# Dealing of token rows by indirect transfers: pairs on two semaphores in place of runs of sixteen

## What is computed

```python
logits = flat @ Wr                                   # 4096 x 8
probs = softmax(logits); topk_p, topk_i = top_k(probs, 2)
topk_p = topk_p / topk_p.sum(-1)
capacity = ceil(n * 2 / 8 * 1.25)                    # 1280
order = argsort(-score, axis=1)[:, :capacity]        # each expert's tokens, heaviest first
dispatch = flat[order]
expert_out = (silu(dispatch @ w1) * (dispatch @ w3)) @ w2 * weight_sel
routed = zeros.at[order].add(expert_out)
out = routed + (silu(flat @ s1) * (flat @ s3)) @ s2  # h + this
```

## Time and profile before

| | us |
|---|---|
| median of 3 runs | 2147.89 (2139.88 to 2156.07) |
| profiled execution | 2143.08, its span 2141.3 |
| granted TensorE clock, mean | 0.939 of full speed |
| busy: TensorE | 1915.5 (89%) |
| busy: VectorE, ScalarE, GpSimd | 1141.0, 739.1, 426.9 |

### The profile page before, as it was taken

The page is one execution under the profiler, slowest core; times in us unless marked ns, Lnnn a source line. Parts: engine busy times, 40 slices in busy tenths (PEclk is TensorE's granted clock), DMA queues, the critical chain, the costliest instruction groups (busy, mean ns, idle before and its releaser), DMA issues. The chain is left out here.

```text
span 2141.3 us, 28066 instructions
## 1 busy us (share of the span) xinstructions
PE 1915.5 (89%) x10075; PEld 1209.1 (56%) x10075; DVE 1141.0 (53%) x2777; ACT 739.1 (35%) x1248; POOL 426.9 (20%) x567
## 2 busy tenths in 40 slices
PE   4985569999999999779999996898799999999997
PEld 2442432444444444446666663555358888888886
DVE  5898668666666765368778873474112222222221
ACT  1434014455545555445655551211011111111111
POOL 5200211022102210201111110103711222222222
PEclk9987568999999999889999997899899999999999
DMA  2610022112111210000000000101221222122321
GB/s 64 223 48 0 1 80 57 52 38 60 53 52 38 60 50 18 26 11 6 6 6 6 6 6 26 74 1 40 80 73 40 69 59 60 32 61 61 68 39 18
DMA packets 68748, 94.75 MB, mean 44 GB/s; under 512 B 15386, under 2 KB 57662, under 8 KB 66337
## 3 DMA queue, kind: packets, MB, share of 16 engines
q1 hardware_dynamic: 52482, 77.19, 11.3%
q0 software_dynamic: 16128, 15.76, 4.3%
HBM read 54.96 MB, written 39.47 MB: 44 GB/s over the span
## 5 line engine op out<-in xcount | busy, mean ns | idle before, releaser
L1028 DVE TENSOR_REDUCE row_max<-c_ps_m 128x1 f32<-128x512 f32 x384 | 253.0, 687 | 112.1 <-PE c_ps_m L1198 106.7
L1376 ACT ACTIVATE e<-c_ps_s 128x512 f32<-128x512 f32 x384 | 216.5, 596 | 220.8 <-PE c_ps_s L1214 220.1
L2675 DVE TENSOR_TENSOR e_f<-e_ps_u,e_gate 128x512 f32<-128x512 f32 x120 | 83.0, 692 | 271.5 <-ACT e_gate L2957 179.1
L2476 POOL DMA_INDIRECT out<-m_o,m_row_of x80 | 125.7, 1572 | 281.9 <-issue 252.7
L2892 PE MATMUL e_ps_o<-m_w,e_f 128*128 128x192 f32 x960 | 162.6, 326 | 0.9 <-DVE e_f L2675 0.9
L2892 PEld LDWEIGHTS e_ps_o<-m_w,e_f 128*128 128x128 f32 x960 | 158.1, 190 | 3.3 <-DVE e_f L2675 1.3
L1198 PE MATMUL c_ps_m<-c_kT,qT 96*128 96x512 bf16 x384 | 150.0, 397 | 10.4 <-DVE row_max L1028 10.2
L1214 PE MATMUL c_ps_s<-qT,c_kT 97*128 97x512 bf16 x384 | 144.6, 386 | 13.1 <-ACT e L1376 5.6
L2957 ACT ACTIVATE e_gate<-e_ps_g 128x512 f32<-128x512 f32 x120 | 71.7, 597 | 242.3 <-PE e_ps_g L2866 162.3
L2860 PE MATMUL e_ps_g<-m_xT,m_w 128*128 128x256 f32 x480 | 129.6, 392 | 1.0 <-DVE h L2507 1.0
L2860 PE MATMUL e_ps_u<-m_xT,m_w 128*128 128x256 f32 x480 | 123.2, 379 | 0.0
(11 more groups left out here) (459 smaller groups left out, 3748.4 us busy)
## 6 DMA issues: line engine op xcount, KB each, us to landing
dealt<-x SPq DMA_DIRECT2D x8, 1290.0 KB, 15.1
m_x<-dealt SPq DMA_DIRECT2D x40, 258.0 KB, 2.7
spread<-parts SPq DMA_DIRECT2D x24, 384.0 KB, 2.3
qT<-spread SPq DMA_DIRECT2D x144, 64.0 KB, 2.5
c_kT<-spread SPq DMA_DIRECT2D x144, 64.0 KB, 2.5
m_w<-in_w13e SPq DMA_DIRECT2D x8, 1152.0 KB, 5.1
m_w<-in_w2e SPq DMA_DIRECT2D x8, 576.0 KB, 6.1
out<-h SPq DMA_DIRECT2D x8, 384.0 KB, 3.9
```

The costliest lines, as they stand in the source:

```text
L1028: dve.tensor_reduce(row_max[:, n // J, n % J:n % J + 1], ps_m[:, n % 2, :], AX_X, ALU.max)\
L1376: act.activation(e[:, n % LIVE_E, :], ps_s[:, n % 2, :], ACT.Exp, scale=QSCALE).then_inc(e_ready, 1)
L2476: pool.indirect_dma_start(out=out_rows, out_offset=bass.IndirectOffsetOnAxis(ap=row_of[:, n % 2, r:r + 1], axis=0), in_=o[:, n % 2, r, :], ...
L2675: dve.tensor_tensor(fe[:, n % 2, 2 * i:2 * i + 2, :], ps_ue[:, q % 2], gate_e[:, q % 2], ALU.mult)\
```

## The change

In place of one semaphore there are two, and pairs of transfers use them in turn: transfers 0 and 1 the first, 2 and 3 the second, 4 and 5 the first again. Before each pair, GpSimd waits until the pair before the previous one has landed, so that at most four transfers are under way. The waits after 16 and after 48 transfers are gone; at the end of each half (k) GpSimd waits for both semaphores. SyncE waits for both too. The count, order and content of the transfers are the same.

```diff
-        scattered = kit.pool_dma_sem("s_scattered")
+        scattered = [kit.pool_dma_sem(f"s_scattered{w}") for w in range(2)]
...
-            sp.wait_ge(scattered, 2 * NB * 16)
+            for w in range(2):
+                sp.wait_ge(scattered[w], NB * 16)
...
                 for b in range(NB):
+                    pair = (k * NB + b) // 2
+                    if b % 2 == 0:
+                        past(pool, scattered[pair % 2], pair // 2 * 32)
                     pool.indirect_dma_start(
                         out=dealt, out_offset=bass.IndirectOffsetOnAxis(ap=slot[:, k, b:b + 1], axis=0),
                         in_=x1[:, b, :], in_offset=None, bounds_check=SLOTS - 1, oob_is_err=False
-                    ).then_inc(scattered, 16)
-                    if (b + 1) % (NB // 2) == 0:
-                        pool.wait_ge(scattered, (k * NB + b + 1) * 16)
-            pool.wait_ge(scattered, 2 * NB * 16)
+                    ).then_inc(scattered[pair % 2], 16)
+                for w in range(2):
+                    pool.wait_ge(scattered[w], (k + 1) * NB // 2 * 16)
```

## The result

| | kernel before | kernel after |
|---|---|---|
| median | 2151.35 us (4 runs, 2139.88 to 2156.07) | 2175.64 us (4 runs, 2172.65 to 2177.42) |
| ratio | | 1.0105, interval 1.0075 to 1.0134 |
| profiled execution, span | 2143.08, 2141.3 us | 2172.65, 2170.9 us |

The change costs 24.3 us between the medians and 29.6 us between the two spans. The profiled execution of the kernel before was one of its quicker ones (2143.08 against a median of 2151.35), which is the main reason why the two differ. The forecast was 2151 us with a range up to 2168; the time lies above it. Lines behind the edit stand 3 to 4 further down in the changed kernel: the transfer is L2454, the gate L2934, the residual L2510, the output matmuls L2753.

What follows compares the result with a forecast made beforehand. TensorE was taken to bound the kernel, with the shared expert 36.0 us late only during GpSimd's dealing. Dealing 0, waits 0, lateness +3 on the 2147.89 us median gave 2151 us, range 2106 to 2168.

Steps and rivals of the forecast that it cites:

- Slack and length of the dealing: GpSimd's 64 row transfers: 84.1 us instead of 88.1, ending near 1559; rows ready 40.4 us before TensorE transposes them, gain 0.
- Cap of four not reached, waits worth 0: New pair waits on GpSimd: each pair's slot comes 2.86 us after pair p-2, landing needs 2.31, so nothing is held back.
- TensorE's lateness: Shared expert beside the dealing, 36.0 us late before because TensorE's signals come late; forecast 37.4 to 41.0, taken as +3 us.
- the check against the 36.0 us: Fit on the kernel before: 0.54 us per us of dealing, two drains counted as pauses, gave 37.8 against 36.0 measured.
- TensorE's 5.59 us of standstill: Gap in TensorE's records from 1493.33, waiting for the gate, ending just after the first drain; cited for the slower rival.
- the slower one: Rival, chance 0.13: signals come through properly only once transfers are drained, and stretches between drains double; +24, 2172 us.
- gates 29 to 31 came through within a run: Sign cited against the slower rival: these ScalarE gates passed during a run of transfers, before a drain.
- The rival of the vanished lateness: Rival, chance 0.20: waits after each pair keep GpSimd's queue short, so all 36.0 us of lateness return; 2112 us.
- The waits bind: Rival, chance 0.12: landing takes over 2.86 us, the dealing gets gaps, roughly half the lateness goes; -18, 2130 us.
- The page's rule: Skill page's statement on DMA and compute engines; by it the change is worth 0, but the sum didn't use it.

Runs made afterwards that it cites:

- e_run32: Kernel before with its drain only after every 32nd transfer and none of the new waits per pair: ratio 1.0105 to the kernel before, 2179.94 us.
- f_cap2: Changed kernel with single transfers on the two semaphores in turn, at most two under way, never drained within a half: 2129.37 us.
- f_plain: Kernel before without the indirect transfers; SyncE copies the same 64 blocks to HBM by plain transfers in pairs: 2109.75 us.
- run 32: Kernel before with waits only after 32 and 64 transfers, run on two chips: 2179.94 us (1.0105) on A, 2109.7 us (1.0001) on B.

## Why the prediction was wrong

**Slack and length of the dealing: right.** Dealing was forecast at 84.1 us and took 84.5. The rows are on GpSimd at 1562.70, and TensorE comes for them some 75 us later.

**Cap of four not reached, waits worth 0: right.** 0.30 us stand before the transfers, with the waits as without them, and e_run32, which has none of the new waits, gives the same ratio.

**TensorE's lateness: wrong, and this is the step that failed.** The prediction took it as a constant rate, 0.54 us lost for each us of dealing, with 4.9 us free at the start and 6.6 us after a pause, and summed 37.4 to 41.0 us, +3. Measured were 67.0, or 0.92 for each us beyond the same two pauses. The rate came from one stretch of 16.3 us within a run of sixteen, and the check against the 36.0 us was weak: it counted two of the three drains as pauses, which made it fit. The loss isn't a rate. It is 0 in runs of eight, 1.0 us in runs of eleven, 9.0 on average in runs of sixteen and 33 to 35 in runs of 32, so a run of 32 isn't a run of sixteen with one free start fewer: its second half is lost whole. The rows gave a hint: TensorE's 5.59 us of standstill stood at the end of the first run, not spread over it.

**The right rival was the slower one, given 0.13.** Its mechanism, that TensorE gets a lead of some 10 us done in each run and then loses the rest, was worked out at about 26 us a half and +16, with a bound of +36.6, and priced between them at +24, 2172 us. The halves cost 33.5 us on average and the lateness grew by 31.0, within the bound; that the medians differ by just 24.3 is luck, since the one profiled execution of before was less late than its median. What it said of the drain is too narrow: f_cap2 shows that distances of 1.73 us do as well, the gate at 1511.63 came through 1.8 us before the half's last transfer was issued, and that at 1538.37 amid the second half. What spoke against it in the prediction, that gates 29 to 31 came through within a run, is true and weighs little: the gates trickle.

**The rival of the vanished lateness failed** because its condition did: it needed pauses that the waits on pairs never made. Its price, 2112 us, is near what kernels with pauses take (2113.65 and 2115.95), where some 45 us came back and not 36, since the kernel before took 2160 us beside them. **The waits bind** didn't happen, but f_cap2 is that case made by hand: pace 1.73 us, all of the lateness gone and not half.

**The page's rule.** The Trainium skill, SBUF — State Buffer, section Who interferes with whom, says that a DMA never contends with a compute engine. f_plain agrees for plain transfers, and so do chips B and C. On chip A and in the pair of before and after, transfers issued by GpSimd at 1.28 us in runs of 16 and 32 went with 36 to 75 us of lateness, 5.9 in runs of eleven and 0 once spaced further. No run shows where the two meet, so it isn't shown that they contend for a port.

**What stays open.** Which property of these transfers delays TensorE's signals: GpSimd's issue, the descriptors, or the scattered writes. The kernels made for it ran only where the effect is absent. That a break without a wait suffices wasn't shown either, for the same reason. Nor was the number of transfers under way parted from their distance. And why one chip has the effect and two have none, or whether it's the occasion, isn't known; in the traces of run 32 on A and B the dealing begins within 0.5 us of each other (1478.18 and 1477.65).

## What to carry to other kernels

Where GpSimd sends a long row of indirect transfers beside TensorE's work, look for waits put down to "remote" and for distances that grow only in that stretch; if they are there, spacing the transfers (here drains of 8 to 11) gave back some 2% on the chip that had the effect, and 1.3 to 1.4% where the spacing made the rows themselves come late (drains of 4, at most two under way). A cap on what is under way did nothing here while landing kept up with the issue it allowed, and a drain that looks like 2 us wasted can be what keeps another engine going. An interference of this kind must be measured on more than one chip: the same edit cost 1.05% on one and nothing that shows on another (1.0001), and the remedy was 0.981 on one and 1.0036 on another.

## What the runs showed of the hardware

- The kernel before takes 2151 to 2161 us on some chips and 2107 to 2110 on others, and on chip A the difference goes with the dealing, a stretch of 88 us: without it the kernel takes 2108.13 us there.
- A transfer that GpSimd issues takes it 0.97 us and the next starts 1.28 us later; with half the rows the distance is 1.21 us, so it hardly hangs on the rows. A drain within a half costs 2.1 to 2.8 us of idle time (once 3.22).
- Beside such transfers on chip A, matmuls without anything to wait for started 2.80 us apart, where 1.0 us is usual at that clock, and a residual started 73 us after the recorded end of the matmuls it waited for.
- With TensorE idle, its granted clock stayed at 0.50 (1.2 GHz) from 1495 to 1512 us, so the first matmuls behind each standstill run at half speed: two gate matmuls took 2.08 us instead of 1.02.
